# Attention and mixture-of-experts block on eight cores: two of four layernorms per token chunk moved from expert unit 13 to the start of the next chunk

## The reference

```
x = x + layernorm(attn(layernorm(x)))        # scores = q k^T / 32, softmax over keys
x = x + layernorm(ffn(layernorm(x)))
ffn(x):
  scores = softmax(x @ gate_w.T)             # 16 experts in 4 groups
  keep 2 groups by their best score, then 4 experts; c = their scores, else 0
  y = sum_e c[:, e] * ((silu(x @ w1[e]) * (x @ w3[e])) @ w2[e])
  z = (silu(x @ ws1) * (x @ ws3)) @ ws2      # shared expert, width 1024
  return y + z
```

## Time and profile before

| what | us |
|---|---|
| times of the two runs shown | 5188.18 and 5761.97 |
| median given | 5475.08 |
| time of the profiled execution | 5190.68 |
| its span, slowest core (core 3) | 5189.1 |
| fastest core of it | 5150.3 |
| PE busy | 4139.7 (80%) |
| DVE busy | 2019.0 (39%) |
| ACT busy | 882.7 (17%) |

### The profile page before, as it was taken

One profiled execution on the slowest core, in us unless ns is written; L12 is line 12 of the kernel. 1 busy time (PEld: TensorE's weight loads), 2 busy tenths in 40 slices (PEclk: granted clock), 3 DMA queues, 4 the chain that ended last, 5 costly groups with the idle time before them and its releaser, 6 DMA issues.

```text
span 5189.1 us, 53931 instructions; the slowest of 8 cores (5150.3 to 5189.1 us)
## 1 busy us (share of the span) xinstructions
PE 4139.7 (80%) x18864; PEld 1922.6 (37%) x18864; DVE 2019.0 (39%) x3050; ACT 882.7 (17%) x1354; POOL 85.7 (2%) x42
## 2 busy tenths in 40 slices
PE   3679856766799789969962679889989979996995
PEld 2334332322344344434421334344444434443442
DVE  2323533333334433443352323543433434344335
ACT  2114122222111111111102114111111111111110
POOL 0000000000000000000010000000000000000001
PEclk7889968887899889979985889989989989997997
DMA  3000458887444334334434000434424433433442
GB/s 130 25 9 5 143 176 281 283 258 257 147 150 170 126 122 155 146 110 158 146 110 142 25 9 5 137 136 153 163 98 151 161 135 115 161 130 123 153 156 104
DMA packets 123565, 695.63 MB, mean 134 GB/s; under 512 B 9620, under 2 KB 9620, under 8 KB 86440
## 3 DMA queue, kind: packets, MB, share of 16 engines
q1 hardware_dynamic: 123304, 692.18, 37.9%
HBM read 601.96 MB, written 90.18 MB: 133 GB/s over the span
## 4 chain that ended last, share of the span: by engine, by line
PE 68%; DVE 12%; DMA 10%; issue 5%; ACT 3%; POOL 1%; DVEq 1%; SPq 0%; ACTq 0%; POOLq 0%
PE PS L33 68%; DMA RV<-w 5%; DVE st L33 3%; DVE RA L33 3%; DVE RK L33 2%; DMA RV<-x1park 1%; DMA RK<-x 1%; DVE c_buf L33 1%; DVE glog L33 1%; ACT RK L33 1%; DVE RW L33 1%; DMA RV<-ws 1%; DVE RV L33 1%; POOL RV L33 1%; DMA RA<-Wq 1%
## 5 line engine op out<-in xcount | busy, mean ns | idle before, releaser
L33 PE MATMUL PS<-RQ,RW 128*128 128x512 bf16 x9216 | 2059.4, 385 | 177.9 <-DVE RW L33 94.8
L33 PEld LDWEIGHTS PS<-RQ,RW 128*128 128x128 bf16 x9216 | 911.1, 99 | 1301.6 <-issue 246.7
L33 PE MATMUL PS<-RW,RK 128*128 128x512 bf16 x4608 | 1076.3, 391 | 330.9 <-DVE RA L33 320.1
L33 DVE SCALAR_TENSOR_TENSOR RA<-PS,c_buf,RA 128x1024 f32<-128x1024 f32 x480 | 613.8, 1283 | 955.9 <-PE PS L33 955.4
L33 PEld LDWEIGHTS PS<-RW,RK 128*128 128x128 bf16 x4608 | 444.5, 100 | 940.5 <-issue 485.4
L33 ACT ACTIVATE RK<-PS 128x512 f32<-128x512 f32 (+1 forms) x608 | 367.0, 620 | 2158.0 <-PE PS L33 2153.3
L33 DVE TENSOR_TENSOR RK<-RK,PS 128x512 bf16<-128x512 f32 x576 | 394.1, 687 | 489.4 <-PE PS L33 489.0
L33 PE MATMUL PS<-identb,RA 128*128 128x128 bf16 x640 | 71.8, 287 | 346.5 <-DVE RA L33 334.1
L33 PE MATMUL PS<-RV,RA 128*128 128x512 bf16 x1024 | 228.9, 384 | 28.4 <-DVE RK L33 14.9
L33 PE MATMUL PS<-RA,RW 128*128 128x512 bf16 x1024 | 241.1, 401 | 8.8 <-DVE RA L33 8.8
L33 PE MATMUL PS<-RK,RQ 128*128 128x512 bf16 x1024 | 221.3, 379 | 3.0 <-DVE RV L33 3.0
(11 more groups left out here) (79 smaller groups left out, 1654.6 us busy)
## 6 DMA issues: line engine op xcount, KB each, us to landing
RW<-wbf SPq DMA_DIRECT2D x126, 2048.0 KB, 7.9
RW<-wbf SPq DMA_DIRECT2D x126, 1024.0 KB, 4.9
RV<-w SPq DMA_DIRECT2D x96, 1024.0 KB, 7.6
wbf<-RW SPq DMA_DIRECT2D x18, 2048.0 KB, 13.8
wbf<-RW SPq DMA_DIRECT2D x18, 1024.0 KB, 7.5
RA<-x SPq DMA_DIRECT2D x32, 512.0 KB, 3.3
RK<-x SPq DMA_DIRECT2D x32, 512.0 KB, 4.2
x1park<-RK SPq DMA_DIRECT2D x32, 512.0 KB, 2.9
```

The lines of the kernel that those rows point to most:

```text
L33: self._last = getattr(self.e, name)(*a, **k)
```

## The change

The second pair of `back_ln` goes from behind unit 13 of a chunk to the next chunk's boundary, behind the last unit's stt and ahead of the four `back_tr`. ACT no longer waits for the squares before its copy, and waits for them instead before the silu instructions of a chunk's first unit. Tile addresses, buffers and the instructions themselves stay as they are.

```
@@ bk_s (ACT, in back_tr)
                         if kb < 2 and b > 0:
                             s.wait(mget(f"b{b - 1}ffn_mm_done"))
-                        if kb >= 4:
-                            s.wait(mget(f"b{b}k{(kb // 4) * 4 + (3 if kb % 2 == 0 else 2)}x1v1"))
                         sl = (kb % 2) * D
@@ us (ACT, in unit_sv)
                             s.wait(mget(f"b{b}U{u - 1}amul{gp}"))
+                            if u > 0 and u % NPE == 0:
+                                s.wait(mget(f"b{b}k{(u // NPE) * 4 + 2 + gp // 2}x1v1"))
@@ loop over g
                         unit_stt(g * NPE - 1)
+                        back_ln(4 * g + 2)
+                        back_ln(4 * g + 3)
                         back_tr(4 * g)
@@ loop over e
-                        if e == 13 and g + 1 < NCH:
-                            back_ln(4 * (g + 1) + 2)
-                            back_ln(4 * (g + 1) + 3)
```

## The result

| | before | after |
|---|---|---|
| median of all runs, us | 5413.55 (10 runs) | 5489.36 (11 runs) |
| lowest | 5188.18 | 5222.15 |
| highest | 5761.97 | 5880.35 |
| profiled execution | 5190.68 | 5230.19 |
| its spans, eight cores | 5150.3 to 5189.1 | 5187.5 to 5228.7 |

The ratio of after to before is 1.007, with a 95% interval of 1.005 to 1.009. In many executions of both kernels the cores of one die (four of the eight), or of both, are granted a lower clock and take longer (in the one of 5880.35 us four cores have 0.76 and need over 5825 us, while the other four have 0.88 to 0.89 and need 5178 to 5218 us); the ratios leave such runs out, and the medians contain them.

What follows compares the result with a forecast made beforehand. Outside dense stretches the kernel was taken as a relay between PE, DVE and ACT. Cost 58.4 us less gain 26.8 us, net 31.6 us on 5190.7 us, gave 5222 us, range 5197 to 5251.

Steps and rivals of the forecast that it cites:

- boundaries g = 1, to the gate matmul: Two chunk boundaries without preceding fin_tile: ACT's tile 0 copy 8.1 us late each, table load included, 16.2 us together.
- boundaries g > 1, to the gate matmul: Four chunk boundaries after fin_tile: no table load, but x1 loads awaited; copy 7.4 to 10.4 us late, 36.6 us together.
- from there to the next chunk's first h1: At the four g > 1 boundaries, tile 0's gate matmul runs 1.4 us slower each, 5.6 us together.
- conversion chunk, unit 13: Unit 13 there loses its layernorm pair, falling from 48.45 to 35.15 us: 13.3 us gained, lower bound 10.9 us.
- unit 13 in five other chunks: In five chunks with ready weights, PE's 2.7 us pause before y's second half goes: 13.5 us gained.
- ACT's queue as the place that decides: At the boundary, ACT's tile 0 copy stands behind both square roots, moving every later step by the same amount.
- The landing of the x1 load: At boundaries with g > 1, the x1 load lands 4.0 us after SP's issue, range 2.9 to 6.8 us; DVE waits.
- The gate matmul at the low clock: At g > 1, tile 0's gate matmul behind some 10 us pause takes 3.56 us, before 2.17 us.
- The moved waits, and the weights behind the loads: ACT's moved waits for squares, and first-unit weights issued some 1 us later at g > 1: both cost nothing.
- Rival A: At g > 1, x1 loads land after 6.8 us, 2.8 us more each: 5233 us; chance 0.13.
- Rival B: At the boundaries, moved layernorms are hidden if ACT's copies go ahead of the roots: 5164 us; chance 0.08.
- Rival C: Longer boundary pause keeps PE's clock low through the next unit's 64 matmuls: 5298 us, 2.1% slower; chance 0.05.

Runs made afterwards that it cites:

- early loads: The change, but SP issues the two x1 loads behind unit 13's weights as before; ratio to before 1.0047, profiled execution 5217.3 us.
- interleaved kernel: Against the change, the boundary's two layernorms stand between the transposes of tiles 0, 1 and 2, squares go to silu_sb; ratio to before 0.9964.

## Why the prediction was right or wrong

The forecast was 5222 us, 0.6% more, in a range of 5197 to 5251. The median of all eleven runs, 5489.36 us, is far outside. The step that failed is the level on which the sum was put, "the profiled execution goes with the shorter, 5188.18, and I forecast for executions like it": I had two runs of before, 574 us apart, took the shorter as what would be measured, and put the spread between runs at nothing but 15 us either side. Of the eleven runs of the changed kernel and the profiled one, five are between 5222 and 5231 us, and seven between 5286 and 5880. The change itself has no part in that: the ten times of the kernel before go from 5188 to 5762 us, with a median of 5413.55. What makes the times of one kernel so different is open; no run here shows it.

On what the change does, the ratio of 1.007 against a forecast of 1.006, the sum stood, in part by luck, as the terms show. They are means over eight cores where not said:

| term | forecast, us | measured, us |
|---|---|---|
| boundaries g = 1, to the gate matmul | 16.2 | 2 x 7.9 = 15.9 |
| boundaries g > 1, to the gate matmul | 36.6 | 38.7 |
| from there to the next chunk's first h1 | 5.6 | 4.6 |
| conversion chunk, unit 13 | -13.3 | 46.9 to 33.7: -13.2 |
| unit 13 in five other chunks | -13.5 | y to y 23.7 to 20.8, five times: -14.9 |
| net | +31.6 | +31.1; mean span +36.1 |

In the five other chunks all pauses of 2.7 us are gone, which is the 13.5 us; the rest is 0.1 us at each and the slower matmuls behind 4 of 40 pauses. Of the 5.0 us between the last two numbers, 2.9 us arise ahead of unit 13 of the conversion chunk and 2.0 us between the last chunk of sequence 0 and the first h1 of sequence 1; the rest nearly cancels. The change moves nothing in either place, and the kernel with only the waits changed is off by more in the first, 4.7 us, so I take these for differences between executions.

- ACT's queue as the place that decides: right. The copy starts 0.14 us behind the second root, and the early loads leave exactly that part.
- The landing of the x1 load, 4.0 us: too short. At the four boundaries of core 4 the reduce began 5.4, 5.9, 4.9 and 5.0 us after SP's issue, and over all cores the load took 5.1 us on average (4.1 to 6.7). That is 4.3 us more over four boundaries; half of it was made good by luck, because SP issued the loads 2.3 us ahead of the last stt's end on average, where the rows of core 3 that I used have 1.8. How late the load starts also varies, as SP's store waits for POOL: in the profile before SP was free 3.5 us ahead of the end of the last stt at the boundary near 4256 us, and after it issued the loads 0.35 us behind that end (4272.66 against 4272.31 us). The four boundaries together cost 43.6 us on core 4 and 32.6 us on core 5; the 38.7 us are the mean of eight.
- The gate matmul at the low clock: right. It takes 3.56 us at the second boundary, where it took 2.17 us.
- The moved waits, and the weights behind the loads, cost nothing: shown for the waits by their own run, in the order of before, and by the rows given there. For the weights, core 4 takes 23.9 us from tile 0's gate matmul to the first h1 at all six boundaries, those with a late load and those without.
- Rival A, a late load, had the right direction: on core 4 the loads are a third to two thirds of the way from 4.0 to 6.8 us.
- Rival B, hidden: false for the change, because ACT kept its order, but true of the work. What I wrote as its condition, copies ahead of roots, is what the interleaved kernel does, and it reached 0.996 where 5164 of 5191 us is 0.995.
- Rival C, the clock: false. From 1341 to 1376 us the granted clock is 0.54, as in the earlier trace rows, and the 64 matmuls behind the boundary took 16.4 us at the first and 15.7 us at the second boundary, far from 28 us.

```profile
1341.00:1376.00 35.00, 20.28 (x95) 18.98 (x96) 8.44 (x17) 10.35 (x22) 0.00 (x0) 0.54 0.18 71
```

This row is the window over the first boundary after, with the columns of the earlier trace rows; the clock is the third number from the end.

The Trainium skill's 1.38 us of drain ("ScalarE: Activation LUTs", section "What ACT_TABLE_LOAD costs") can now be put to a cleaner test than before: the early-load kernel has the same chain with a table load at g = 1 and without one at g > 1, 10.52 and 9.24 us. The difference is 1.28 us, the load alone. ACT had been idle before the load there, but no drain shows behind work either: in the profile before (core 3) ten loads start 0.02 us behind a square root and three 0.02 us behind a CAST of 1.90 us, and each time the next instruction starts 0.01 us behind the load's end. Here the measurement decides against the page's 1.38 us.

## What to carry to other kernels

Work that is "only moved" is priced by the queue in which it stands, on every engine it touches: a root of 0.2 us for tile 3 held back the copy of tile 0, because both are ACT's and the root waits for DVE. Put such a step behind what the next engine already waits for, in pieces short enough to fit beside it: in the chunks with ready weights a layernorm of 6 us beside h1 was free, and a pair of 10.9 us stuck out by 2.7; in the conversion chunk even a single one cost 7 us. And issue the load where it stood when only its consumer moves.

## What the runs showed that I had not expected

How even a boundary is when no DMA is in it: 9.24 us on 8 cores at 4 boundaries within 0.02 us, while with the load in the chain it is 9.4 to 15.5 us. A switch of ACT's table costs the 1.28 us of its load and nothing more, whether ACT had been waiting before it or working. And a pause of PE of some 3 us can cost 1.4 us on top of itself, when the granted clock falls to 0.71 behind it.
